# Two transformer blocks on one core: five projections as 16-bit passes, a new order of jobs, and another head

## What is computed

```python
# block 0, 8 heads of 40
hs = mha(x @ Wq, enc @ Wk, enc @ Wv)                       # "FIRST": 124 context rows
ca_hs1 = mha(ca_q1, x, x)                                   # "CA": queries from the 4 tokens
ca_hs2 = mha(ca_hs1 @ Wq, ca @ Wk_ca, ca @ Wv_ca)           # 4 keys
x = (hs + ca_hs2) @ Wout + b_out + x
# block 1, 20 heads of 16
x = attn(ln(x), ln(x), q1, k1, v1) @ o1 + x                 # "SELF"
x = attn(ln(x), context, q2, k2, v2) @ o2 + x               # "CROSS"
a, g = split(ln(x) @ ff_w1 + ff_b1); x = (a * gelu(g)) @ ff_w2 + ff_b2 + x
```

## Time and profile before

| what | us |
| --- | --- |
| median of 3 runs (lowest to highest) | 3948.45 (3946.22 to 3966.26) |
| the profiled execution, its own time | 3965.49 |
| its span, first to last instruction | 3963.6 |
| busy in the span: PE / PEld | 3580.9 / 2867.6 |
| busy in the span: DVE / ACT / POOL | 2308.9 / 2268.7 / 1966.4 |

### The profile page before, as it was taken

How to read it: one execution, slowest core, us unless ns; L and a number is a source line. 1 busy time by engine, 2 the same in 40 slices (tenths; PEclk the granted TensorE clock), 3 DMA queues, 4 the chain that set the end, 5 groups by cost and what they waited for, 6 DMA issues and landing times.

```text
span 3963.6 us, 112057 instructions
## 1 busy us (share of the span) xinstructions
PE 3580.9 (90%) x38314; PEld 2867.6 (72%) x38314; DVE 2308.9 (58%) x5535; ACT 2268.7 (57%) x4084; POOL 1966.4 (50%) x2229
## 2 busy tenths in 40 slices
PE   6499999999999999999999999999999999999999
PEld 5377777777777777777777777777777777777777
DVE  6466556556555655655556556555655656556555
ACT  2356655665556556556655665566566556655664
POOL 0345444554555445555554554545445555554553
PEclk9799999999999999999999999999999999999999
DMA  4332333222233332232333322233332232333321
GB/s 138 63 61 53 58 61 66 59 46 60 59 55 61 67 61 49 53 65 51 63 63 66 59 46 60 56 58 61 67 64 47 53 64 53 63 63 66 59 46 42
DMA packets 417600, 238.71 MB, mean 60 GB/s; under 512 B 44315, under 2 KB 416715, under 8 KB 416843
## 3 DMA queue, kind: packets, MB, share of 16 engines
q1 hardware_dynamic: 405317, 229.62, 29.6%
q10 hardware_dynamic: 11910, 3.04, 0.3%
HBM read 153.50 MB, written 79.06 MB: 59 GB/s over the span
## 4 chain that ended last, share of the span: by engine, by line
PE 36%; issue 30%; POOL 17%; DVE 5%; SPq 4%; DMA 3%; ACT 3%; POOLq 1%; ACTq 0%; DVEq 0%
PE bank L1412 35%; POOL PT L519 10%; DMA xin<-in_x 3%; DVE mx L1025 2%; ACT PT L742 2%; POOL cQ L526 2%; POOL XA L496 1%; POOL cK L526 1%; SPq L365 1%; POOL rstd L566 1%; SPq L363 1%; POOL XB L496 1%; PE bank L1446 1%; PE bank L1531 1%; SPq L361 1%
## 5 line engine op out<-in xcount | busy, mean ns | idle before, releaser
L519 POOL TENSOR_TENSOR PT<-P,PT 128x512 f16<-128x512 f32 (+1 forms) x924 | 1068.8, 1157 | 642.1 <-ACT PT L742 640.8
L1412 PE MATMUL bank<-hT,w_ff_w 128*128 128x256 f16 x5440 | 651.6, 277 | 1.7 <-DVE hT L1054 1.7
L1025 DVE TENSOR_REDUCE mx<-bank 128x4 f32<-128x512 f32 (+1 forms) x924 | 579.6, 680 | 104.4 <-PE bank L1412 96.5
L1412 PEld LDWEIGHTS bank<-hT,w_ff_w 128*128 128x128 f16 x5440 | 532.5, 100 | 73.2 <-issue 6.5
L1412 PE MATMUL bank<-mxs,pick 84*128 84x128 f16 (+1 forms) x3696 | 513.4, 220 | 0.0
L1412 PE MATMUL bank<-w_ff,F 128*128 128x320 f32 x1360 | 411.5, 442 | 1.3 <-DVE F L1104 1.3
L1412 PEld LDWEIGHTS bank<-mxs,pick 84*128 84x128 f16 (+1 forms) x3696 | 375.1, 103 | 16.8 <-issue 8.2
L1412 PEld LDWEIGHTS bank<-V,PT 128*128 128x128 f16 (+1 forms) x9504 | 314.5, 96 | 84.0 <-POOL PT L519 37.9
L723 ACT ACTIVATE P<-bank,ff_b,scale 128x256 f32<-128x256 f32 x340 | 187.8, 562 | 324.9 <-PE bank L1412 285.4
L1412 PE MATMUL bank<-Qs,Ks 96*128 96x128 f16 x2640 | 361.7, 220 | 0.1
L1412 PE MATMUL bank<-V,PT 128*128 128x17 f16 (+1 forms) x9504 | 343.7, 172 | 17.1 <-POOL PT L519 14.3
(11 more groups left out here) (274 smaller groups left out, 7295.4 us busy)
## 6 DMA issues: line engine op xcount, KB each, us to landing
Ks<-scratch_k SPq DMA_DIRECT2D x198, 160.0 KB, 4.5
Qs<-scratch_q SPq DMA_DIRECT2D x198, 160.0 KB, 5.7
scratch_k<-cK SPq DMA_DIRECT2D x134, 128.0 KB, 1.8
scratch_q<-cQ SPq DMA_DIRECT2D x134, 128.0 KB, 2.1
Q0s<-scratch_q SPq DMA_DIRECT2D x99, 160.0 KB
K0s<-scratch_k SPq DMA_DIRECT2D x99, 160.0 KB
cT<-in_cT SPq DMA_DIRECT2D x136, 96.0 KB, 2.0
xin<-in_x SPq DMA_DIRECT2D x34, 320.0 KB, 3.2
```

What stands on the lines that cost most here:

```text
L519: nc.gpsimd.tensor_tensor(PT[0:keys, n % PT_SLOTS, 1, :], P[0:keys, n % P_SLOTS, :], PT[0:keys, n % PT_SLOTS, 0, :], ALU.subtract).then_in ...
L1025: nc.vector.tensor_reduce(mx[:, g % 2, 4 * u:4 * u + 4], bank[:, :].rearrange("p (h s) -> p h s", h=4)[:, :, 0:keys], axis=AX.X, op=ALU.ma ...
L1412: return nc.tensor.matmul(o, lhsT, rhs, start=start, stop=stop)
```

## The change

The five float32 projections become float16 passes: eight for Q0T (`PASSES_X`), five for K0T, K2T, V0 and V2 (`PASSES_C`). Their weights are split in the head like the others. The inputs are split each step: ACT scales xT in place and writes two high parts (`split_x`, in the pass before, behind gelu(9) and `next_factors`), POOL writes the low part (`low_x`, ahead of low_probabilities(14)); the same for the context (`split_context` behind exps(3), `low_context` behind low_probabilities(3)). K2T now uses this pass's context, so the second context buffer is gone. gelu's output has a buffer of its own. The orders of jobs and of all five engines' lists are new: among others the CA scores lie ahead of K1T, V2 among the CROSS and FIRST units, y0 ahead of T14, y1 after T27, the bias additions elsewhere, and attends stand in other places among the T's. In the head, M4 is formed first and stored in quarters by ACT, half of the feed-forward shifts come ahead of the turn of the largest weights, the largest are found in one reduce each, and Qs, Ks, cQ and cK are cleared by POOL while DVE clears X4, XA, XB, OA, OB and hT3. Core of the diff (a line of "..." is where lines are left out; the last parts are PE's list):

```diff
-MATS0 = ("Wq",)
-MATSC = ("Wk", "Wv", "Wv_ca", "k2", "v2")
+MATSC = ("Wv_ca",)
+MATSX, MATSK = ("Wq",), ("Wk", "Wv", "k2", "v2")
+MATS16 = MATSN + MATSX + MATSK
+BLOCKS = {n: 2 if n in MATSK else 3 for n in MATS16}
+PASSES_C = ((1, 0, 0), (3, 0, 0), (1, 1, 0), (2, 0, 1), (2, 1, 1))
+PASSES_X = ((1, 0, 0), (1, 1, 0), (4, 0, 0), (2, 0, 1), (2, 1, 1), (5, 0, 1), (3, 0, 2), (3, 1, 2))
+ROWS_X, AT_X = (64, 128, 128), (128, 0, 192)
...
 BODY = jobs_of("""
-    Q0T0 XT0_0 Q0T1 XT0_1 Q0T2 K1T0 K1T1 K1T2 Q1T0 Q1T1 Q1T2 S0 S1 V0_0 V1_0 mx0 S2 S3 T0 K0T0 T1
-    V1_1 mx1 K0T1 T2 S4 S5 S6 S7 S8 T3 vca mx2 S9 S10 T4 S11 S12 T5 S13 caT0 T6 mx3 T7 T8 caT1 K0T2
-    T9 T10 T11 T12 T13 V0_1 outT1_0 ff0 ff1 outM1_0 outT1_1 ff2 ff3 outM1_1 XT1_0 ff4 s4 XT1_1 ff5
-    Q2T0 Q2T1 Q2T2 ff6 ff7 mT ff8 mB ff9 S14 S15 S16 S17 y1 S18 S19 mx4 S20 S21 S22 T14 S23 K2T0 T15
-    mx5 S24 T16 S25 T17 T18 T19 T20 S26 T21 mx6 T22 outT2_0 S27 y0 T23 p4T T24 mx7 T25 outM2_0 K2T1
-    T26 hs0 T27 outT2_1 V2_0 outT0_0 hs1 K2T2 outM2_1 outT0_1 XT2_0 V2_1 outM0_0 outM0_1 XT2_1 G
+    XT0_0 Q0T0 Q0T1 S0 S1 XT0_1 Q0T2 S2 S3 K1T0 mx0 K1T1 K1T2 Q1T0 mx1 Q1T1 Q1T2
+    T0 V1_0 T1 T2 V1_1 T3 vca K0T0 K0T1 caT0 caT1
+    S4 S5 S6 K0T2 S7 S8 V0_0 mx2 S9 S10
+    T4 S11 T5 S12 V0_1 T6 S13 s4 T7 mx3 T8 K2T0 T9 K2T1 T10 T11 outT1_0 T12 outM1_0 T13
+    ff0 ff1 ff2 outT1_1 ff3 outM1_1 ff4 p4T ff5 XT1_0 XT1_1 ff6 Q2T0 Q2T1 Q2T2 mT ff7 mB ff8 ff9
+    S14 S15 S16 S17 S18 y0 mx4 S19 S20
+    T14 S21 T15 K2T2 T16 S22 T17 S23 T18 mx5 T19 S24 T20 S25 T21 mx6 T22 outT2_0 T23 S26 V2_0
+    T24 outM2_0 T25 S27 mx7 V2_1 T26 outT2_1 T27 outM2_1 hs0 outT0_0 hs1 y1 outM0_0 outT0_1 XT2_0 XT2_1 outM0_1 G
...
+            def load_step(i):
+                for half in (0, 64):
+                    sp.dma_start(xT[half:half + 64, 0, :], d["xT"][i, 128:192, :]).then_inc(step_loaded, 16)
+                    sp.dma_start(cT[half:half + 64, 0, :], d["cT"][i, 128:192, :]).then_inc(step_loaded, 16)
+                sp.dma_start(xT[:, 1, :], d["xT"][i, 0:128, :]).then_inc(step_loaded, 16)
+                sp.dma_start(xT[:, 2, :], d["xT"][i, 192:320, :]).then_inc(step_loaded, 16)
+                sp.dma_start(cT[:, 1, :], d["cT"][i, 0:128, :]).then_inc(step_loaded, 16)
                 sp.dma_start(ca32[:, :], d["caG"][i, :, :]).then_inc(step_loaded, 16)
                 sp.dma_start(carep[:, :, :], d["carep"][i, :, :].rearrange("(k p) n -> p k n", p=96)).then_inc(step_loaded, 16)
                 sp.dma_start(xin[:, :, :], d["x"][i, :, :, :].rearrange("g s c -> s g c")).then_inc(step_loaded, 16)
...
             def load_next(i):
-                sp.wait_ge(v_done, v_job(i, LOOP_JOBS, "V0_1"))
+                sp.wait_ge(v_done, v_job(i, LOOP_JOBS, "vca"))
+                sp.wait_ge(c16_ready, i + 1)
...
-                load_step(i + 1, i)
+                load_step(i + 1)
...
                 stack_self(i)
                 put_low(i, "K0T", 0, cK, CH0, s_k0, AT0, k0_put, self_stacked)
-                stack_cross_keys(i)
                 put_low(i, "K0T", 1, cK, CH0, s_k0, AT0, k0_put)
                 put_low(i, "K0T", 2, cK, CH0, s_k0, AT0, k0_put)
-                load_next(i)
                 stack_first_queries(i)
                 stack_first_keys(i)
+                load_next(i)
+                stack_cross_keys(i)
                 put_split(i, "Q2T", 0, cQ, s_q2, q2_put, first_stacked)
                 put_split(i, "Q2T", 1, cQ, s_q2, q2_put)
                 put_split(i, "Q2T", 2, cQ, s_q2, q2_put)
                 stack_cross_queries(i)
+                put_out(i, 0, stores)
                 put_low(i, "K2T", 0, cK, CH1, s_k2, AT1, k2_put, cross_stacked)
                 put_low(i, "K2T", 1, cK, CH1, s_k2, AT1, k2_put)
-                put_out(i, 0, stores)
+                put_low(i, "K2T", 2, cK, CH1, s_k2, AT1, k2_put)
                 put_out(i, 1, stores)
-                put_low(i, "K2T", 2, cK, CH1, s_k2, AT1, k2_put)
...
+            def low_x(i):
+                pool.wait_ge(x_high, i + 2)
+                nc.gpsimd.tensor_tensor(x16[:, 3:6, :], xT[:, :, :], x16[:, 0:3, :], ALU.subtract).then_inc(x16_ready, 1)
+            def low_context(i):
+                pool.wait_ge(c_high, i + 1)
+                nc.gpsimd.tensor_tensor(c16[:, 2:4, :], cT[:, :, :], c16[:, 0:2, :], ALU.subtract).then_inc(c16_ready, 1)
...
+            nc.gpsimd.memset(M4_part[:, :, :, :], 0.0).then_inc(M4_clear, 1)
+            pool.wait_ge(low_ready, 1)
+            for landed in M4_put:
+                pool.wait_ge(landed, 16 * 2)
+            pool.wait_ge(M4_last, 16)
+            pool.wait_ge(M4_clear, 1)
+            for t in (Qs, Ks):
+                nc.gpsimd.memset(t[:, :, :], 0.0)
+            pool.drain()
+            for t in (cQ, cK):
+                last = nc.gpsimd.memset(t[:, :, :, :], 0.0)
+            last.then_inc(cleared, 1)
+            pool.wait_ge(cleared, 2)
...
             token_queries(-1)
+            low_x(-1)
...
                 low_probabilities(i, 2)
                 low_probabilities(i, 3)
+                low_context(i)
+                zero_bias(i, 0)
...
+                second_bias(i, 0)
+                second_bias(i, 1)
                 low_split(i, "Q2T", 0, cQ)
                 low_split(i, "Q2T", 1, cQ)
                 low_split(i, "Q2T", 2, cQ)
+                token_queries(i)
                 x_values(i, 0, OA)
                 x_values(i, 1, OA)
-                token_queries(i)
+                low_x(i)
                 low_probabilities(i, 14)
...
                 low_probabilities(i, 16)
-                second_bias(i, 0)
...
+            def split_x(i):
+                act.wait_ge(step_loaded, i * LOADS_STEP + 2 * LOADS_STEP)
+                act.wait_ge(next_ready, i + 2)
+                act.wait_ge(j_full, done(i, LOOP_JOBS.number("Q0T2"), "J"))
+                nc.scalar.activation(xT[:, :, :], xT[:, :, :], ACT.Copy, scale=next_factor[:, SX:SX + 1])\
+                    .then_inc(x_scaled, 1)
+                act.wait_ge(x_scaled, i + 2)
+                nc.scalar.activation(x16[:, 0, :], xT[:, 0, :], ACT.Copy, scale=lower[:, :])
+                nc.scalar.activation(x16[:, 1:3, :], xT[:, 1:3, :], ACT.Copy).then_inc(x_high, 1)
+            def split_context(i):
+                act.wait_ge(step_loaded, i * LOADS_STEP + LOADS_STEP)
+                act.wait_ge(factor_ready, i + 1)
+                act.wait_ge(j_full, done(i - 1, max(LOOP_JOBS.number("K2T2"), LOOP_JOBS.number("V2_1")), "J"))
+                nc.scalar.activation(cT[:, :, :], cT[:, :, :], ACT.Copy, scale=factor[:, SC:SC + 1])\
+                    .then_inc(c_scaled, 1)
+                act.wait_ge(c_scaled, i + 1)
+                nc.scalar.activation(c16[:, 0, :], cT[:, 0, :], ACT.Copy, scale=lower[:, :])
+                nc.scalar.activation(c16[:, 1, :], cT[:, 1, :], ACT.Copy).then_inc(c_high, 1)
...
                     act.wait_ge(v_done, v_job(i, jobs, f"ff{t - 2}"))
-                elif t == 0:
-                    act.wait_ge(low_p, units_done(min(i, STEPS) if isinstance(i, int) else i, LAST_UNIT[SELF, 1]))
+                else:
...
-                if n == LAST_UNIT[SELF, 1] + 1:
-                    act.wait_ge(v_done, v_job(i, LOOP_JOBS, f"ff{FFT - 1}"))
...
+            act.wait_ge(M4_clear, 1)
+            for q in range(4):
+                if q >= 2:
+                    act.wait_ge(M4_put[q % 2], 16)
+                    act.wait_ge(M4_last, 16)
+                for k, r in enumerate(CH0):
+                    act.wait_ge(M4_ready, 3 * q + k + 1)
+                    nc.scalar.activation(M4_part[0:r, q % 2, k, :], j_bank[4 + (3 * q + k) % 2][0:r, :], ACT.Copy)\
+                        .then_inc(M4_copied, 1)
+                act.wait_ge(M4_copied, 3 * q + 3)
+                act.dma_start(s_M4[q * 8:(q + 1) * 8, :, :, :].rearrange("s p k n -> p k s n"),
+                              M4_part[:, q % 2, :, :].rearrange("p k (s n) -> p k s n", s=8)).then_inc(M4_put[q % 2], 16)
+                if q == 0:
+                    act.dma_start(s_M4[STEPS, :, :, :], M4_part[:, 0, :, 0:G * HEADS0 * T4]).then_inc(M4_last, 16)
             act.wait_ge(amax_ready, 1)
...
-                gelu(i, L, 6)
                 gelu(i, L, 7)
                 gelu(i, L, 8)
+                gelu(i, L, 9)
                 next_factors(i, L)
-                gelu(i, L, 9)
+                split_x(i)
                 load_exp_table()
                 high_maxima(i, 4)
-                exp4(i)
                 exps(i, 14)
-                high_chunk(i, "K2T", 0, cK, CH1[0], FK2)
                 exps(i, 15)
-                high_maxima(i, 5)
+                high_chunk(i, "K2T", 2, cK, CH1[2], FK2)
                 exps(i, 16)
                 exps(i, 17)
                 exps(i, 18)
+                high_maxima(i, 5)
                 exps(i, 19)
                 exps(i, 20)
                 exps(i, 21)
@@ -877,19 +955,17 @@
...
+            def chunk(i, name, c, wn, src, passes, at, rows):
```

(40 more changed lines are left out.)

550 lines of the change are left out of this document (251 added, 299 removed).

## The result

The changed kernel takes 4730.9 us (median of 4 runs, 4724.9 to 4733.0), the kernel before 3948.9: a ratio of 1.197, 95% interval 1.193 to 1.200. The forecast had the side right and the size wrong: 4225 us, range 3800 to 4390.

What follows compares the result with a forecast made beforehand. PE seemed the bound, but joints showed DMA, ACT and DVE ending most stretches. From the profiled 3965.5 us, 33 passes at +9.0 less 22 for the head gave 4240, on the median's side 4225 us; range 3800 to 4390.

Steps and rivals of the forecast that it cites:

- The pair of 3.9 us: SELF: T(n+2) behind attend(n) on PE makes two exps cost 3.9 us, though they take ACT 2.7.
- POOL's lag: ff9 to CROSS: later next_factors and added low_x make exps(16) wait for POOL, starting at 15.5 us instead of 12.7.
- Rival 1: Whole pass: PE stays the bound in every stretch, 3759 us, or 3840 with half the saving lost; chance 0.24.
- I count about two fifths of them: +9.0: Per-pass sum: only part of the 3.9 us of least sure waits counted, so +11.4 became +9.0 us.
- The walk: Following each stretch's chain in the new order: a pass of 126.9 us against 115.5, +11.4.
- placed waits: Waits from order: 1.0, 0.9 and 0.8 us in SELF, 1.2 in CROSS, 3.9 together.
- The last attend to K1T: 15.1: End of a pass: y1's products, projections and DVE's residual, norms and maxima take 15.1 us, before 14.5.
- exps(16) to the last exponential: 21.3: CROSS: 19.5 us becomes 21.3, with 0.6 for moves on ACT and 1.2 for exps(19) waiting on mx5.
- S4 to ff9, 48.8: SELF and feed-forward: pairs and waits put exps(13) at 25.3 us; the stretch takes 48.8 instead of 46.1.
- I leave this out of the sum: PE's clock in SELF: if it falls, four pairs lengthen by 3.2 us; kept as a rival, not summed.
- rival 3: SELF and CROSS: the clock falls, +12 to +16 us a pass, 4320 to 4450 us; chance 0.14.
- The head: Before the passes: first K1T at 136.5 us instead of 158.7, 22 gained, between 8 and 35.

Runs made afterwards that it cites:

- g_first: Changed kernel with G's low part taken ahead of norm(0, 1) in DVE's list instead of behind it: 4626.2 us.
- cross_order: Changed kernel with two exchanges in CROSS, mx5 ahead of T18 and T23 ahead of outT2_0: 4640.9 us.
- before_pairs: Kernel before with each attend(n) in SELF ahead of T(n+2) in PE's list: 4292.5 us, ratio 1.087.
- old_lists_early_split: Changed kernel with the kernel before's job order and engine lists, few departures, context split right behind Q1T2: 3949.4 us, ratio 1.0004.
- the filler: Changed kernel with six 128-column matmuls that nobody reads ahead of each attend's wait: 4703.6 us.
- The four edits: Changed kernel with T(n+2) ahead of attend(n), G's low part early, POOL's path to CROSS shortened, two CROSS jobs exchanged: 4393.2 us.
- my three further sets of orders: Changed kernel with four order edits plus T13, S26, S27, mx7 earlier; or the end's order; or work ahead of S4: 4463.4, 4422.5, 4425.2 us.
- all of them together: Changed kernel with all the order edits, plus mx0 and mx1 behind Q1T2: 4520.3 us.

## Why the prediction was right or wrong

- **The side, and the mechanism: right.** Order, not work, sets the time. The pair of 3.9 us is there (4.0 to 4.2), S4 waits for the stack, POOL's lag puts exps(16) at 15.1 us after ff9 (15.5 said), PE's idle time grew. Rival 1, PE as the bound, is out: 5.9 us more of its work cost 1.1.
- **"I count about two fifths of them: +9.0": wrong.** The walk gave +11.4, and I took 2.4 off, since its placed waits (3.9 together) seemed least sure. They came to 5.2 in the pass read. Against pairs of 3.9 us, s4 cost 0.9 (exps(5) to exps(7) 4.75; placed 1.0), T8's maxima 0.3 (exps(6) to exps(8) 4.18; placed 0.9), T13 2.3 (exps(11) to exps(13) 6.24; placed 0.8), and exps(19) came 3.1 behind exps(18) instead of some 1.4, 1.7 more (placed 1.2). Two were smaller than placed and two larger.
- **"The last attend to K1T: 15.1": wrong by 3.8.** I did not look up whose bank Q0T0 takes, nor that G's low part had moved behind norm(0, 1). g_first: 3.15 us a pass.
- **"exps(16) to the last exponential: 21.3": 24.3** (1202.05 to 1226.4). Against the kernel before, exps(19) lost 1.6, exps(23) behind the turn of outT2_0 1.1, exps(24) 1.0 and exps(26) 1.0. The walk had 1.2 for the first and 0.6 for all else. cross_order, which took out the first two, gave 2.9 us a pass.
- **S4 to ff9, 48.8: 51.3.** exps(13) came 27.0 us after S4 instead of 25.3: exps(4) was 0.9 late already (6.5 instead of 5.6), and the pairs and waits add 0.8. The other 0.8 lie behind.
- **The clock, "I leave this out of the sum": wrong.** The range of rival 3 (+12 to +16 a pass) was the nearest, and still short of 23.5. The doubled price of a wait shows in g_first and before_pairs. The change and old_lists_early_split do the same float16 work in different orders: of the 23.6 us a pass between them 12.8 are idle time of PE and 10.8 are longer matmuls. How much of the 10.8 a pass really waited for stays open: the filler raised the clock and gave back 27 us of 782, but it had to put its own work in.
- **One pass for the mean.** The walked pass of before is 1.1 us over its mean, that of after 1.4 under: 2.5 us that a comparison of two passes hides. With the misses of the stretches (9.6) and the discount (2.4) this makes the 14.5 between +9.0 and +23.5.
- **The head: 10.0 us gained, not 22.** Scales were due at about 70 and came at 81.5: ACT issues M4's stores itself, and was held 10.5 us behind the first quarter (8.9 by the issue of the store for the last step) and 6.3 us ahead of the third, until a store had landed. PE's products of M4, ahead of its shifts, waited 10.0 and 4.8 us for ACT. Q0T0 then waited 5.4 us for low_x, which stands behind POOL's values and token queries. POOL's clearing did not delay these: it ended 5.1 us before next_factors came (130.02).

The four edits account for 10.1 of the 23.5 us, by measurement. The other 13.4 are shown to lie in the new orders (old_lists_early_split has all the rest of the change and is level), but not in which of their waits: my three further sets of orders, and all of them together, found none.

## What to carry to other kernels

In lists that engines work off in order, a forecast needs the queue walked for every job that moved, its bank's last reader too. Waits that one is unsure of should not be discounted as a group: these came to 5.2 us where 3.9 were placed and 1.5 counted. Work taken from the busiest engine buys nothing by itself if the order leaves that engine without work at the next wait: here PE's idle time behind DVE's maxima grew by 4.3 us a pass, while 5.9 us of added work cost 5.1. A single pass can mislead on where time goes (2.2 us in one pass, 0.6 on average), so sum the waits over all passes. To judge such a change, put the new parts into the old lists first; that one run told more than all partial edits.

## What was not expected of the hardware

A wait is paid twice when the clock falls behind it: the same 16 matmuls took 3.59 us behind a wait of 2.53, and 1.96 behind one of 0.74. The Trainium skill (TensorE: Matmul & The Clock Gate, HAM oscillation) describes it: PE stops for a wait and starts the next group at the lower clock. The traces agree: with one edit of order the clock lay at its lower level, 0.50, for some 20 us of the pass read (before_pairs), where it had been full. The way out that the section gives is a loop order in which PE does not stop. Filler is not its advice, and it did not pay here: 0.856 to 0.937 of clock for 27 us, and in two other places a loss of 35 and 57.
